# One more copy on VectorE, one pass on GpSimd: re-dividing the small work between the batches of an attention kernel

## The reference

```
x = x + attention(layernorm(x), ctx)      # 16 heads of 32, causal, keys and values from ctx
x = x + ffn(layernorm(x))                 # shared SwiGLU of width 704 and, for each token,
                                          # 2 of 8 experts of width 352, weighted by a softmax
```

## Time and profile before

| what | value |
|---|---|
| median of 3 runs | 372.49 us (370.49 to 372.67) |
| the profiled execution | 370.16 us |
| its span, first to last instruction | 368.3 us |
| mean granted TensorE clock | 0.989 of full speed |
| busy share of PE, DVE, ACT, POOL over the whole span | 92%, 69%, 64%, 25% |

### The profile page before, as it was taken

The page is one execution under the profiler, slowest core; times in us unless marked ns, Lnnn a source line. Parts: engine busy times, 40 slices in busy tenths (PEclk is TensorE's granted clock), DMA queues, the critical chain, the costliest instruction groups (busy, mean ns, idle before and its releaser), DMA issues.

```text
span 368.3 us, 6770 instructions
## 1 busy us (share of the span) xinstructions
PE 340.6 (92%) x2192; PEld 275.8 (75%) x2193; DVE 255.7 (69%) x460; ACT 234.2 (64%) x611; POOL 91.0 (25%) x106
## 2 busy tenths in 40 slices
PE   5599899898999999999999999999999999999971
PEld 5477777676677588798896788888887887888750
DVE  2994886888875518782676797778778778777810
ACT  3525988999995422512226287887887888888720
POOL 3648222322231000054600002211311311221131
PEclk9899999999999999999999999999999999999997
DMA  7999000000000669995779743443354344344233
GB/s 228 365 368 368 17 2 2 3 2 0 3 3 2 239 205 394 372 381 202 253 248 209 266 128 82 64 79 85 59 85 86 57 76 90 64 68 79 52 40 46
DMA packets 28457, 49.45 MB, mean 134 GB/s; under 512 B 6672, under 2 KB 11792, under 8 KB 27408
## 3 DMA queue, kind: packets, MB, share of 16 engines
q1 hardware_dynamic: 24288, 39.91, 33.0%
q0 software_dynamic: 4144, 9.23, 14.2%
HBM read 32.22 MB, written 16.92 MB: 133 GB/s over the span
## 4 chain that ended last, share of the span: by engine, by line
PE 69%; ACT 13%; DVE 7%; DMA 5%; issue 3%; POOL 1%; POOLq 0%; SPq 0%; ACTq 0%; DVEq 0%
PE bank L495 29%; PE bank L774 21%; PE bank L789 9%; ACT prob L876 8%; DMA out<-y_sb,dest 3%; PE bank L678 2%; ACT probT L831 2%; PE bank L664 2%; PE bank L796 2%; DMA w_kv<-wkvT 2%; DVE x2T_lo L1088 1%; DMA w_sg<-sguT 1%; PE bank L487 1%; PE bank L710 1%; PE bank L709 1%
## 5 line engine op out<-in xcount | busy, mean ns | idle before, releaser
L1088 DVE TENSOR_TENSOR gu_parts<-w_gu,gu_parts 128x704 fp32r<-128x704 f32 x84 | 72.8, 887 | 22.9 <-ACT gu_parts L831 21.4
L831 ACT ACTIVATE gu_parts<-w_gu 128x704 fp32r x84 | 66.1, 790 | 15.0 <-PE bank L774 14.6
L774 PE MATMUL bank<-gu_parts,xsT_hi 128*128 128x352 f32 x336 | 69.8, 329 | 0.0
L476 POOL DMA_INDIRECT out<-y_sb,dest x21 | 33.0, 1571 | 147.9 <-ACT y_sb L1028 143.9
L774 PEld LDWEIGHTS bank<-gu_parts,xsT_hi 128*128 128x128 f32 x336 | 55.3, 189 | 0.5 <-issue 0.5
L774 PE MATMUL bank<-gu_parts,xsT_lo 128*128 128x352 f32 x168 | 40.8, 324 | 0.0
L789 PE MATMUL bank<-w_dn,actT_plain 128*128 (+1 forms) x84 | 39.6, 592 | 0.0
L495 PE MATMUL bank<-x2T_hi,w_sg_lo 128*128 128x512 f32 (+1 forms) x88 | 32.2, 366 | 0.1
L495 PE MATMUL bank<-x2T_hi,w_sg_hi 128*128 128x512 f32 (+1 forms) x88 | 32.0, 363 | 0.0
L495 PE MATMUL bank<-x2T_lo,w_sg_hi 128*128 128x512 f32 (+1 forms) x88 | 31.9, 362 | 0.0
L774 PEld LDWEIGHTS bank<-gu_parts,xsT_lo 128*128 128x128 f32 x168 | 29.3, 189 | 0.0
(11 more groups left out here) (191 smaller groups left out, 749.9 us busy)
## 6 DMA issues: line engine op xcount, KB each, us to landing
w_gu<-guT SPq DMA_DIRECT2D x8, 1408.0 KB, 9.5
xs_dram<-xs_in SPq DMA_DIRECT2D x1, 5460.0 KB, 20.4
xs_in<-xs_dram SPq DMA_DIRECT2D x21, 256.0 KB, 2.6
w_dn<-dnT SPq DMA_DIRECT2D x8, 512.0 KB, 6.2
w_sg<-sguT SPq DMA_DIRECT2D x10, 256.0 KB, 5.7
xres<-x SPq DMA_DIRECT2D x2, 768.0 KB, 9.5
w_dn<-dnT SPq DMA_DIRECT2D x8, 192.0 KB, 6.5
w_sd<-sdnT SPq DMA_DIRECT2D x5, 256.0 KB, 6.8
```

Of the source, the lines that this page charges most:

```text
L476: pool.indirect_dma_start(out=out[:, :], out_offset=bass.IndirectOffsetOnAxis(ap=dest[:, i, 0:1], axis=0), in_=y_sb[i % 2][:, :], in_offse ...
L774: ins = pe.matmul(dst[:, 0:F], xsT[x_][:, c, :], gu2[w_][:, c, f0:f0 + F], start=c == 0 and n == 0, stop=c == C - 1 and n == 2)
L831: act.activation(dst, src, ACT.Copy).then_inc(s[sem], 1)
L1088: dve.tensor_tensor(lo_, src, hi_.bitcast(F32), ALU.subtract).then_inc(s[sem], 1)
```

## The change

For tiles 0 to 4, GpSimd applies the second norm (new `apply2` on its queue, behind `rstd` and ahead of the scaling of groups 2 and 3). VectorE still does tiles 5 and 6, tile 5 behind `oT_lo` of the last batch. VectorE copies the values of all batches from 1 on, ahead of `oT_lo` instead of behind it, and both come ahead of the scaling of group 1. ScalarE no longer copies any but the first batch's values. ScalarE copies `x2T_hi` behind the exponentials of group 0 instead of behind the third `probT`, and VectorE makes `x2T_lo` between the masks of groups 2 and 3 instead of behind both. The queues of TensorE and SyncE stay as they are.

```diff
             for n in range(NB):                                  # GpSimd
                 if n >= 3:
                     rstd(n - 3, "st2", var2, rstd2, mv2, "rs2a", "rs2b")
+                    apply2(n - 3)
                 for r in range(RP, R):
                     normalised(n, r)
...
                 if b + 1 < NB:                                   # ScalarE
                     exps(b + 1, 0)
+                if b >= 3:
+                    put_x2T(b - 3, CC)
                 for r in range(2 if b == 0 else 1, R):
                     put_pT(b, r)
-                    if r == 2 and b >= 3:
-                        put_x2T(b - 3, CC)
...
                 if b + 1 < NB:
-                    if b >= 2:
-                        put_v(b + 1)
                     exps(b + 1, 2)
...
                     masked(b + 1, 2)                             # VectorE
+                if b >= 3:
+                    x2T_lo(b - 3, CC)
+                if b + 1 < NB:
                     masked(b + 1, 3)
...
-                if b >= 3:
-                    x2T_lo(b - 3, CC)
...
+                    put_v(b + 1)
+                oT_lo(b)
+                if b == NB - 1:
+                    apply2(NX - 2)
+                if b + 1 < NB:
                     normalised(b + 1, 1)
-                if b >= 2:
-                    apply2(b - 2)
-                oT_lo(b)
-                if b + 1 < NB:
-                    if b < 2:
-                        put_v(b + 1)
                     normalised(b + 1, 2)
```

More of the change, by code:

```diff
@@ L443, in _, with apply2 @@
             pool.iota(token, [[P, NX], [0, 1]], base=0, channel_multiplier=1).then_inc(s["tok"], 1)
+            def apply2(n):
+                pool.wait_ge(s["rs2b"], n + 1)
+                pool.tensor_scalar(x2n[:, n, 0:H], xres[:, n, :], mv2[:, n, 0:1], rstd2[:, n, :],
+                                   ALU.subtract, ALU.mult).then_inc(s["x2n"], 1)
             for n in range(NB):
```

## The result

| what | before | changed | ratio (95% interval) |
|---|---|---|---|
| first comparison, medians (4 runs each) | 371.91 us | 367.24 us | 0.989 (0.9852 to 0.9927) |
| second, 5 rounds | 371.43 | 368.2 | 0.9909 (0.9875 to 0.9942) |
| third, 5 rounds | 371.62 | 368.28 | 0.9905 (0.988 to 0.993) |

The changed kernel is faster by 0.9 to 1.1%, 3.2 to 4.7 us in the three comparisons. All three lie just at the 1% that I drew between "within" and "faster" (I had given "faster" 28%). The profiled execution took 366.31 us, with a span of 364.5, against 370.16 and 368.3.

A forecast was written before the change was run, and what follows sets the result against it. The stage's per-batch chain, 9.53 us through TensorE, ScalarE and VectorE, was taken as the bound. Gains of 2.59 + 0.22 + 0.35 = 3.16 us, off the median 372.49, gave 369.3, range 367.0 to 372.3.

The forecast's parts named there:

- faster: Whole kernel: faster by over 1% (3.7 us), 28%; within 1% got 68%, slower by over 1% 4%.
- four ScalarE turns: ScalarE, `oT_hi` of batch 2 to batch 6: 38.07 us falls to 35.48, 2.59 less, without the value copy.
- PV further ahead of `oT_hi`: TensorE: PV, freed from `x2T_lo`, runs 1.25 ahead of `oT_hi`, not 1.03; batch 6's PV comes 0.22 earlier.
- batch 7: No exponentials, TensorE the bound: its wait for `x2T_lo`, under half a microsecond, goes; 0.35 counted as gained.
- group 1 until `oT_hi` could start, 1.49: Step of ScalarE's new 8.82 us turn: 85.33 to 87.05 less the 0.23 of waiting.
- VectorE's slack: Next batch's row maximum: ready on VectorE at PV + 4.90, wanted by ScalarE at 5.07; 0.17 a turn.
- Rival C: VectorE becomes the bound, its row maximum late; 0.5 beyond the slack leaves 1.5 of the gain, 371.3 us; 16%.
- GpSimd's norm: Norm on GpSimd takes T = 0.9 us, bounds 0.47 and 1.17; ready at PV + 3.8, hidden.
- T less 1.30 in each of four turns: Cost if GpSimd's norm, T long, holds up VectorE's scaling of group 1; nothing until T = 1.30.
- rival D: Slower through GpSimd's norm holding VectorE's scaling: gain used up at T = 2.1, over 1% lost from 3.0; 6%.
- Rival B: More than 3.7 us gained; ScalarE's own work alone, 8.47 a turn, would give 4.8, or 367.7 us; 28%.
- Rival E: A later stage takes the gain back, 372.5 us: expert loads could end when they did; 5%.

The follow-up runs named there:

- v_g: Changed kernel with `x2T_hi` and `x2T_lo` put back where they were before: 368.58 us against 371.46 for the kernel before, ratio 0.9918.
- v_x: Changed kernel with the second norm back on VectorE for all tiles: 369.9 us against 371.46 for the kernel before, ratio 0.9969.
- g_twice: Changed kernel with GpSimd applying each norm of tiles 0 to 4 twice: 377.05 us against 371.43 for the kernel before, ratio 1.0141.
- the middle version: Changed kernel with `x2T_hi` between `probT` 1 and 2, `x2T_lo` behind both masks; run twice: 368.24 and 367.01 us, ratios 0.9909 and 0.9891 to before.
- g_only: Kernel before with only the norm of tiles 0 to 4 moved to GpSimd: 371.85 us against 371.62, ratio 1.0007.
- after_again: The changed kernel run again, unchanged: 368.2 us against 371.43 for the kernel before, ratio 0.9909.
- v_only: Kernel before with only the value copy moved to VectorE, the norm still on VectorE: 368.38 us against 371.46, ratio 0.9927.
- x_only: Kernel before with only `x2T_hi` and `x2T_lo` sooner: 370.95 us against 371.46, ratio 0.999.
- g_forms: Changed kernel with another form of GpSimd's norm instruction for each of the first five tiles, output wrong: stage 44.56 us, no whole time used.
- mid_again: Second run of changed kernel with `x2T_hi` between `probT` 1 and 2, `x2T_lo` behind both masks: 367.01 us against 371.62 before, ratio 0.9891.
- mid_lo_late: First run of changed kernel with `x2T_hi` between `probT` 1 and 2, `x2T_lo` behind both masks: 368.24 us against 371.43 before, ratio 0.9909.

## Why the prediction came out

The mechanism was right for ScalarE: a turn without the value copy and its two waits, PV freed, a new wait of 0.31 before `probT` 3 (about 0.4 forecast). It was wrong for GpSimd, as told below. By term:

| term | forecast | measured | from |
|---|---|---|---|
| four ScalarE turns | 2.59 | 3.03 | 38.07 less 35.04 |
| PV further ahead of `oT_hi` | 0.22 | 0.12 | 85.11 less 83.96 is 1.15, not 1.25; 1.03 before |
| batch 7 (this is what x2T sooner brings; v_g has 9.90) | 0.35 | 0.45 | 9.92 less 9.47 |
| sum | 3.16 | 3.60 | 48.11 less 44.51 |

*The mis-sized term* is "group 1 until `oT_hi` could start, 1.49". It measures 1.31 (83.80 to 85.11). I had subtracted the wait of 0.23 from a step between two starts, but an engine's next start comes before the end of the instruction in front, and the profile counts a wait from that end: the overlap, some 0.18, stayed in the step. In four turns that is 0.72; the other steps of a turn were together 0.07 too short, which gives back 0.28. The same slip is in PV's lead of 1.25.

*VectorE's slack*, forecast at 0.17, is smaller still: about 0.06 between the row maximum and ScalarE's start (80.18 and 80.24, where 80.18 is an estimate, half of a row of two). Rival C did not happen in the changed kernel, and v_x shows that it does with 0.54 more on that queue. In the prediction I costed the norm's move only as part of this slack, and the table bears that out.

*GpSimd's norm is where I was wrong and lucky.* Its duration, 2.08, was outside my bounds. By my own formula, T less 1.30 in each of four turns, that would have cost 3.1 and left nothing of the gain: rival D at its break-even of T = 2.1. It cost nothing, since the step on which D stood, that VectorE's scaling of group 1 is held until GpSimd's norm has ended, does not occur: it ran in 0.62 inside the 2.08 here, and in 0.62 to 0.80 in g_twice. The Trainium skill, SBUF — State Buffer, section SBUF: two separate sides, would have had the second of the two blocked for the whole first instruction; the hold of the earlier trace rows beside a cast agrees with that, this pair does not, but for the norm's first 0.6 us (last section). The two errors cancelled. What the norm can cost is decided by TensorE's `t2`, 0.36 behind its end, which I had only said "comes later still": g_twice moved the loss there.

*Rival B*, more than 3.7, was met by the medians of the first comparison (4.67), not by those of the other two (3.2 and 3.3), and nearly by the stage (3.60). Its bound for ScalarE's own work, 8.47 a turn, holds the same slip, since two waits are subtracted from a step there too: the middle version takes 34.28 in four turns, against 33.9, but two of the four last only 8.38 (76.72 to 85.10 and 93.76 to 102.14, `oT_hi` to `oT_hi`). *Rival E* is excluded: expert loads start as much sooner as the last projection.

*Two slips outside the sum.* In rival C, 0.5 beyond the slack leaves 1.2 of the gain by its own price of 0.4 for each 0.1, not 1.5; the time given, 371.3, goes with 1.2. In rival D the rows vary 2.5-fold per column (0.92 and 2.28 ns), not fourfold.

*The median* fell 0.6 us further in the first comparison than stage and head start explain together, and 0.3 to 0.4 less than the stage's gain in the other two. One source of this scatter was seen at the other end of the program, below.

## What to carry to other kernels

When three engines have turns of nearly the same length, price edits together and not one by one: relieving the engine that is not late is worth nothing alone (0.01 here), and half of the gain once the other two edits stand and make it late (1.85 of 3.60). Count the last turn by itself too, where another engine is the bound: an edit that is worth 0.06 in the steady turns brought 0.43 there. For an operation that moves to GpSimd, a duration by columns of another form is no bound, so time the very form first, and compare it with the cover in front of its first reader, not of its last. Build a turn from steps start to start throughout, and at a wait take a step from a turn in which there is none; never subtract the wait.

## What the hardware showed beyond that

**GpSimd's forms differ 3.4-fold for the same 512 columns** (0.61 to 2.08), and its two-operation `tensor_scalar` takes 3.8 times VectorE's 0.54. The Trainium skill, GPSIMD Engine Reference, section 3.1 (Elementwise), has 0.77 for 512 elements in the best case, a tight loop; no form here but the copy is that fast.

**Who holds whom between VectorE and GpSimd depends on the instructions and on when they start.** VectorE's scaling with two inputs from SBUF took 0.62 where it started 0.71 to 0.79 after GpSimd's norm of 2.08. It took 0.80 and 0.78 where it started 0.45 after it, and 0.72 where it started 0.52 after it (g_twice; v_g has one more turn of the first kind, 0.45 and 0.80). Start and loss together give 0.61 to 0.63 each time, so I estimate that GpSimd's norm holds this scaling for its first 0.62 us and not for the rest. The other way round, GpSimd's `rstd` of one column takes 0.79 to 0.81 beside the scaling of group 0 and 0.55 without it (v_x at 115.90), and its norm 2.17 in g_only, where VectorE's scaling had started 0.41 before it. But VectorE's norm is held to the end, and not only by the cast of the earlier trace rows. VectorE and GpSimd of the kernel before:

```profile
15.74 2.50 DVE L1081 TENSOR_SCALAR xn<-xres,mv,rstd 128x512 f32<-128x512 f32 x1
```

```profile
15.60 2.36 POOL L417 TENSOR_TENSOR w_q_lo<-w_q,w_q_hi 128x1024 fp32r<-128x1024 f32 x1
```

It ends 0.28 after GpSimd's subtraction, as it did after the cast. VectorE's norm beside GpSimd's norm was not tried.

**The end of the program scatters by more than a microsecond.** The last four down products, TensorE of two profiles of the same changed kernel (the first one, then after_again), in order of time, and the stretch from 355 to 360 in both (columns as above):

```profile
355.18 1.88 PE L795 MATMUL bank<-w_dn,actT_plain 128*128 x4
```

```profile
356.71 3.51 PE L795 MATMUL bank<-w_dn,actT_plain 128*128 x4
```

```profile
355.00:360.00 5.00, 2.06 (x6) 0.71 (x4) 0.00 (x0) 0.69 (x1) 1.56 (x1) 1.00 0.21 37
```

```profile
355.00:360.00 5.00, 4.12 (x8) 1.67 (x7) 0.49 (x2) 0.60 (x3) 0.00 (x0) 0.66 0.40 52
```

With a granted clock of 0.66 in the mean, between the levels of 2.4 and 1.2 GHz, the same four products take 3.51 instead of 1.88. In both executions TensorE had waited about 2.0 just before, 1.1 for VectorE's `act_e` and 0.9 for ScalarE's `actT_split_hi`, so that these waits alone do not decide it. From the end of the last gate-and-up product to that of the last down product it is 5.1 to 5.2 in the profiles of before, after, v_only, x_only, g_forms and mid_again, and 6.7 to 6.9 in those of the other eight, mid_lo_late among them, which is the same kernel as mid_again. What decides it stayed open. For a change worth 3 us in one stage, the length of that stage in the trace tells more than the device time does.
